# Message stage of a graph network: when VectorE adds two finished pair sums, between or behind the products of the next two pairs

## Chip, cores and metric

The kernel runs on one core of a Trainium2 chip (trn2). The metric is the device time of one execution in microseconds, the median of several runs. Everything is float32 except a few small index helpers.

## The reference, cut to what matters

The program is a chain of four blocks on 3125 nodes with 256 features: a graph layer, a mixture of experts, a second graph layer (messages along 53125 edges), and a second mixture of experts, each added to its input. The change lies in the second graph layer alone:

```python
h = silu(edge_scalars @ fc_w1 * (1.0 / sqrt(NES))) * SILU_NORM
w_a, w_b, w_c, w_d = split(h @ fc_w2 * (1.0 / sqrt(FCN)), 4)     # 64 weights of each kind per edge
xg0, xg1 = y0[edge_src], y1[edge_src]                            # 64 scalars and 64 x 3 vectors of the source node
mid0 = w_a * xg0 * ea0
mid1 = w_b * einsum('euc,ec->eu', xg1, ea1) * INV_SQRT3
mid2 = (w_c * xg0)[:, :, None] * ea1[:, None, :]
mid3 = (w_d * ea0)[:, :, None] * xg1
agg = segment_sum(concatenate([mid0, mid1, mid2, mid3]), edge_dst)   # 53125 edges -> 3125 nodes
```

The edges are sorted by their destination. An earlier stage has stored the weights of each edge in DRAM (`edge_w`), and another the transformed node rows (`y_dram`).

## The kernel before

`sum_messages` (from L1865) is one of the kernel's stages. The nodes are cut into 25 tiles of 125, the edges into 208 blocks of 256 (`NB`), 128 partitions with two edges each. A **pair** is one block together with one tile into which some of its edges go; there are 232 pairs (`NPAIR`), since a block that straddles two tiles makes two. A **step** `s` handles pairs `2s` and `2s+1`, so there are 116 steps (`NST`), and five engines work on them at once:

- **GpSimd (POOL)**, L1936 to L1948: gathers the source rows, two indirect DMAs per block (L1940), 416 in all, into a ring of 32 blocks (`got`). Behind every second block it waits for the landing of two blocks that it issued earlier and adds two to `blocks_in` (L1934). Block `b` waits for `made >= (b - 6) // 2` (L1938).
- **SP**, L1907 to L1917: loads the edge weights of both pairs into one of four buffers `w`, behind `made` and `scaled_made` of the step that last used it.
- **ScalarE (ACT)**, L1954 to L1963: twelve scaled copies of the step's mask (L1961).
- **TensorE (PE)**, L1968 to L1984: sixteen float32 matmuls per step (four at L1978, twelve at L1982; the profile lists two records for each) that sum the products of each pair into one of six PSUM banks `ps_z`. It waits for `scaled_made`, for `made`, and for the sums of step `s-3` to have been added (`added`), because those free the banks.
- **VectorE (DVE)**, L2030 to L2048, in order, in iteration `s`: the mask of step `s+1` (L1993, which waits until PE has finished step `s-3`); the six products of step `s` (`products`, L2000: for each pair one instruction at L2010 and two at L2012), behind a wait for the weights, for both blocks (`blocks_in` against `need[1]`, L2004) and for PE; then the two additions of step `s-3` into `agg` (`add_sum`, L2016, the instruction at L2022). Each addition waits for the one before it (`added`, L2019), since both may go to the same tile.

Two registers per iteration hold the tiles to which the sums go, and two more the blocks that the next step reads (`value_load`, L1998 and L2037). The sequencer of VectorE loads them ahead of the instructions that need them; it also carries out the waits that stand in front of an instruction.

The lines that the change and the prediction speak of are L1934, L1938, L1940, L1978, L1982, L1993, L2000 to L2014 and L2016 to L2045.

Of the kernel before, what the change touches and what calls it, by code (L numbers as in the profile page):

```python
# [25 lines left out]
KC = 2  # L26
# [13 lines left out]
MUL = 64  # L40
# [5 lines left out]
ALU, ACT, AX = mybir.AluOpType, mybir.ActivationFunctionType, mybir.AxisListType  # L46
ds = bass.ds
# [100 lines left out]
def row(buf, at, lo=0, hi=None, parts=P):  # L148

    return buf[0:parts, ds(at, 1), lo:hi].rearrange("p o d -> p (o d)")  # L150
# [1714 lines left out]
def sum_messages(nc, k):  # L1865


    RING, LAG = 32, 3
# [3 lines left out]
    RS, MB, ZB, XB = 4, 4, 6, 3  # L1872
# [3 lines left out]
    NST = NPAIR // 2  # L1876
    assert NST * 2 == NPAIR
    with Phase(nc, "msg") as ph:
        FACTOR = C_X / math.sqrt(20.0) / math.sqrt(2 * MUL)
        raw, raw_zero, raw_in = k.up_w, ph.sem("raw_zero"), ph.sem("raw_in")  # L1880
        got = ph.sb("got", [128, RING, KC, 4, MUL])
        lent, used = k.x_sb[:, G:T, :].rearrange("p t d -> p (t d)"), [0]

        def borrow(n):
# [14 lines left out]
        w_in, got_in, blocks_in = ph.sems("w_in", RS), ph.sems("got_in", RING), ph.sem("blocks_in")  # L1899
        rest, rested = ph.sb("rest", [128, 32]), ph.sem("rested")  # L1900
        masked, scaled_made, made, summed, added = (
            ph.sem(x) for x in ("masked", "scaled_made", "made", "summed", "added"))
        block = ph.ctx.enter_context(nc.Block())

        @block.sync
        def _(sp):
            for s in range(NST):  # L1907
                if s >= RS:
                    sp.wait_ge(made, s - RS + 1)
                    sp.wait_ge(scaled_made, s - RS + 1)  # L1910
                if s == 1:
                    sp.wait_ge(k.x_put, 32 * (NG - 1))
                for h in range(2):
                    n = 2 * s + h
                    need = sp.value_load(k.pair_need[0:1, n:n + 1], min_val=1, max_val=NB)
                    sp.dma_start(w[s % RS][:, KC * h:KC * h + KC, :].rearrange("p u w -> p (u w)"),
                                 k.edge_w[ds((need - 1) * SB, SB), :].rearrange("(p u) w -> p (u w)", u=KC)).then_inc(w_in[s % RS], 16)  # L1917
            sp.wait_ge(raw_zero, 1)
            w00, w01, w10, w11 = k.L1_gnn_lin2_w00, k.L1_gnn_lin2_w01, k.L1_gnn_lin2_w10, k.L1_gnn_lin2_w11
            for q, (wa, wb) in enumerate([(w00, w11), (w11, w11), (w01, w10), (w10, w10)]):  # L1920
                sp.dma_start(raw[0:MUL, q, 0:MUL], wa).then_inc(raw_in, 16)
                sp.dma_start(raw[MUL:128, q, MUL:128], wb).then_inc(raw_in, 16)
            sp.wait_ge(summed, LAST + 1)
            for i in range(1, NG):
                for a, b in SPANS:
                    sp.dma_start(k.x_sb[a:b, i * G:i * G + G, :], k.x_dram[i * W:i * W + W, :].rearrange("(j p) d -> p j d", p=P)[a:b, :, :])\
                      .then_inc(k.x_back[i], 16)
# [58 lines left out]
        @block.vector  # L1986
        def _(dve):
            def mask(s):
                if s == 1:
                    dve.wait_ge(k.x_put, 32 * (NG - 1))  # L1990
                if s >= MB:
                    dve.wait_ge(summed, s - MB + 1)
                dve.tensor_tensor(plain[s % MB][:, :, :], ps_lanes[:, :].unsqueeze(1).to_broadcast([128, CH, P]),  # L1993
                                  k.pair_dst[:, 2 * s:2 * s + 2, :].rearrange("p n u -> p (n u)").unsqueeze(2)
                                  .to_broadcast([128, CH, P]), ALU.is_equal).then_inc(masked, 1)

            def place(n):
                return dve.value_load(k.pair_need[0:1, n:n + 1], min_val=1, max_val=NB)  # L1998

            def products(s, need):  # L2000
                p = prod[s % XB]
                v = w[s % RS][:, :, 0:D].rearrange("p c (k v) -> p c k v", v=MUL)
                dve.wait_ge(w_in[s % RS], 32 * (s // RS + 1))
                dve.wait_ge(blocks_in, need[1])  # L2004
                if s >= XB:
                    dve.wait_ge(summed, s - XB + 1)
                for h in range(2):
                    y = got[:, ds(need[h] % RING, 1), :, :, :].rearrange("p o u k v -> p (o u) k v")
                    at = slice(KC * h, KC * h + KC)
                    dve.tensor_tensor(p[:, at, 0:8:7, :], v[:, at, 0:4:3, :], y[:, :, 0:1, :].to_broadcast([128, KC, 2, MUL]), ALU.mult)  # L2010
                    for q in (1, 2):
                        last = dve.tensor_tensor(p[:, at, 3 * q - 2:3 * q + 1, :], v[:, at, q:q + 1, :].to_broadcast([128, KC, 3, MUL]),  # L2012
                                                 y[:, :, 1:4, :], ALU.mult)
                last.then_inc(made, 1)  # L2014

            def add_sum(n, tile):  # L2016
                if n % 2 == 0:
                    dve.wait_ge(summed, n // 2 + 1)
                dve.wait_ge(added, 1 + n)  # L2019
                if n == 0:  # L2020
                    dve.wait_ge(rest_zero, 1)
                dve.tensor_tensor(row(k.agg, tile), ps_z[n % ZB][0:P, :, :].rearrange("p k v -> p (k v)"), row(k.agg, tile), ALU.add)\  # L2022
                   .then_inc(added, 1)

            dve.memset(raw[:, :, :], 0.0).then_inc(raw_zero, 1)
            dve.wait_ge(lanes_made, 1)
            dve.memset(k.agg[:, 0:T // 2, :], 0.0).then_inc(added, 1)
            mask(0)
            need = [place(0), place(1)]
            for s in range(NST + 3):  # L2030
                if s + 1 < NST:
                    mask(s + 1)
                if s < NST:
                    products(s, need)
                if s >= 3:
                    first, second = 2 * s - 6, 2 * s - 5
                    tile = [dve.value_load(k.pair_tile[0:1, n:n + 1], min_val=0, max_val=T - 1) for n in (first, second)]  # L2037
                if s + 1 < NST:
                    need = [place(2 * s + 2)]
                if s >= 3:  # L2040
                    add_sum(first, tile[0])
                if s + 1 < NST:
                    need.append(place(2 * s + 3))
                if s >= 3:
                    add_sum(second, tile[1])  # L2045
                if s == NST - 1:
                    dve.wait_ge(raw_in, 128)
                    dve.tensor_scalar(k.up_w[:, :, :], raw[:, :, :], FACTOR, None, ALU.mult)  # L2048
# [520 lines left out]
```

## Time and profile before

| what | us |
|---|---|
| median of three timed runs | 1999.07 |
| lowest and highest of them | 1993.88, 2004.77 |
| span of the profiled execution | 2413.3 |
| message stage in the profiled execution, 1248 to 2058 | 810 |
| stage of the first graph layer in it, 75 to 725 | 650 |

The profiled execution is one run in which each instruction is recorded; its span, from the first to the last instruction, is 414 us longer than the median of the timed runs, which are not recorded. Durations of single instructions and the order of events are read from it; how its length stands to the timed runs has to be argued. In the profile's rows "idle before" is the time the engine stood still in front of an instruction, and the name behind the arrow is what ended it: an engine with its line, "issue" where nothing in the profile held it, "remote" where the signal came from no instruction that the profile could match.

### The profile page before, as it was taken

What the parts mean: (1) busy time and instruction counts of PE and PEld (TensorE: products, weight loads), DVE (VectorE), ACT (ScalarE), POOL (GpSimd) and SP (SyncE); (2) the same over time, 40 slices, a digit from 0 to 9 for tenths busy, and PEclk for the clock granted to TensorE, in tenths of its full rate; (3) what the DMA queues carried; (4) which work ended last, traced back from release to release, by engine and by line L of the source; (5) the groups of instructions that cost most, each with busy time, mean ns of one, the idle gap of its engine ahead of it and who ended that gap; (6) DMA issues with size and microseconds to landing.
All of it is one profiled execution on the core that took longest, in us unless ns stands there. A gap on an engine that the chain in (4) does not pass through costs nothing. (4 is left out here: it accounts for less than half of the span.)

```text
span 2413.3 us, 38460 instructions
## 1 busy us (share of the span) xinstructions
PE 1891.3 (78%) x9911; PEld 1517.9 (63%) x9911; DVE 1125.8 (47%) x2791; ACT 1021.4 (42%) x3052; POOL 1104.5 (46%) x1499
## 2 busy tenths in 40 slices
PE   1368787877799858999455877787778789899699
PEld 1245454554466657999335766676767679777588
DVE  3532222222242374544664666565656669431322
ACT  2513343343353532333264555454545557454222
POOL 5547667666700004555375665565655550000243
PEclk7679999889999858999777888887888889999799
DMA  5636556565734026666544554555554553255553
GB/s 150 202 90 198 190 187 198 185 193 187 210 140 138 11 64 201 212 212 215 135 149 147 150 159 140 151 155 145 147 153 144 150 148 107 69 164 177 155 180 129
DMA packets 229197, 376.43 MB, mean 156 GB/s; under 512 B 66081, under 2 KB 114308, under 8 KB 228998
## 3 DMA queue, kind: packets, MB, share of 16 engines
q1 hardware_dynamic: 174820, 222.13, 31.0%
q0 software_dynamic: 52224, 150.15, 20.2%
q8 instruction: 89, 1.46, 0.2%
q10 hardware_dynamic: 1954, 1.79, 0.2%
q14 instruction: 110, 0.90, 0.1%
HBM read 275.38 MB, written 99.57 MB: 155 GB/s over the span
## 5 line engine op out<-in xcount | busy, mean ns | idle before, releaser
L1940 POOL DMA_INDIRECT msg_got<-y_dram,block_src x416 | 412.4, 991 | 293.5 <-DVE msg_prod L2012 139.7
L439 POOL DMA_INDIRECT ffn_w<-xn_dram,block_src x384 | 364.6, 949 | 219.2 <-issue 81.7
L1961 ACT ACTIVATE msg_scaled<-msg_plain,msg_w 128x125 f32<-128x125 f32 x1044 | 314.0, 386 | 280.1 <-DVE msg_plain L1993 234.6
L554 PE MATMUL sum_ps_bank<-ffn_w,sum_onehot 128*125 x928 | 270.5, 419 | 115.6 <-DVE sum_onehot L893 84.3
L554 PEld LDWEIGHTS sum_ps_bank<-ffn_w,sum_onehot 128*125 128x125 f32 x928 | 184.0, 206 | 264.6 <-issue 246.6
L881 DVE TENSOR_TENSOR agg<-sum_ps_bank,agg 125x256 f32 x232 | 98.4, 424 | 432.4 <-PE sum_ps_bank L554 216.5
L541 PE MATMUL sum_ps_bank<-sum_fc,sum_space 128*128 128x512 f32 x416 | 231.9, 644 | 68.9 <-ACT sum_space L639 48.3
L650 ACT ACTIVATE sum_space<-sum_ps_bank,sum_rec 128x128 f32<-128x128 f32 x416 | 131.0, 369 | 330.4 <-PE sum_ps_bank L541 159.5
L1982 PE MATMUL msg_ps_z<-msg_prod,msg_scaled 128*125 128x128 f32 x1416 | 207.5, 293 | 53.7 <-issue 53.0
L1982 PEld LDWEIGHTS msg_ps_z<-msg_prod,msg_scaled 128*125 128x125 f32 x1416 | 198.6, 206 | 72.4 <-issue 64.1
L2022 DVE TENSOR_TENSOR agg<-msg_ps_z,agg 125x512 f32 x232 | 159.4, 687 | 23.9 <-issue 5.2
L1978 PE MATMUL msg_ps_z<-msg_prod,msg_plain 128*125 128x256 f32 x472 | 142.1, 420 | 31.9 <-issue 20.0
L2439 POOL DMA_INDIRECT last_rows<-ffn_rows,ffn_token x32 | 30.8, 963 | 289.2 <-SPq L78 279.7
L1533 ACT ACTIVATE ffn_run_hid<-ffn_run_ps_h,cols 128x128 f32<-128x128 f32 x256 | 73.2, 368 | 178.9 <-issue 134.6
L1993 DVE TENSOR_TENSOR msg_plain<-msg_ps_lanes,pair_dst 128x500 f32<-128x500 f32 x87 | 58.5, 672 | 190.6 <-remote 183.6
L1961 ACT ACTIVATE x_sb<-x_sb 128x125 f32<-128x125 f32 x348 | 104.0, 385 | 93.4 <-DVE x_sb L1993 77.2
L541 PEld LDWEIGHTS sum_ps_bank<-sum_fc,sum_space 128*128 128x128 f32 x416 | 76.0, 205 | 93.5 <-ACT sum_space L639 53.8
L1490 PEld LDWEIGHTS ffn_run_ps_h<-ffn_run_rows_t,ffn_run_w 128*128 128x128 f32 x1024 | 125.9, 194 | 5.0 <-DVE ffn_run_rows_t L1575 1.8
L1490 PE MATMUL ffn_run_ps_h<-ffn_run_rows_t,ffn_run_w 128*128 128x128 f32 x1024 | 126.6, 277 | 1.0 <-DVE ffn_run_rows_t L1575 1.0
L1982 PE MATMUL msg_ps_z<-x_sb,msg_scaled 128*125 128x128 f32 x672 | 100.1, 292 | 29.9 <-issue 29.7
L1504 PE MATMUL ffn_run_ps_r<-ffn_w,ffn_run_hid 128*128 x512 | 121.0, 379 | 0.0
L2012 DVE TENSOR_TENSOR msg_prod<-msg_w,msg_got 128x384 f32<-128x384 f32 x236 | 120.2, 550 | 0.0
(343 smaller groups left out, 3397.9 us busy)
## 6 DMA issues: line engine op xcount, KB each, us to landing
edge_w<-sum_space SPq DMA_DIRECT2D x52, 1040.0 KB
msg_w<-edge_w SPq DMA_DIRECT2D x174, 260.0 KB
ffn_run_w<-in_L_ffn_w SPq DMA_DIRECT2D x64, 512.0 KB
x_sb<-edge_w SPq DMA_DIRECT2D x58, 260.0 KB
ffn_rows<-agg SPq DMA_DIRECT2D x25, 448.0 KB
ffn_w<-in_L_ffn_w SPq DMA_DIRECT2D x16, 512.0 KB, 8.7
wd<-in_L_ffn_Wd SPq DMA_DIRECT2D x8, 1024.0 KB, 8.6
msg_got<-y_dram,block_src POOLq DMA_INDIRECT x416
```

Source lines behind the costliest of these rows:

```text
L439: pool.indirect_dma_start(got[:, (b + 1) % RING, u, :], None, k.x if b < RAW else k.xn_dram, bass.IndirectOffsetOnAxis(ap=k.block_src[:, b ...
L541: pe.matmul(ps_w[q % WB][:, :, :].rearrange("p u d -> p (u d)"), hid[g % 2][:, b, :], fc2[:, :, :, :].rearrange("p u k v -> p (u k v)"), s ...
L554: last = pe.matmul(ps_sum[n % ZB][0:P, :], onehot[n % OB][:, u, :], got[:, ds(need % RING, 1), u, :].rearrange("p o d -> p (o d)"), start= ...
L650: act.activation(to[:, b, u, 0:128], ps_w[q % WB][:, u, 0:128], ACT.Copy, scale=r[:, b, u, 8:9])
L1490: last = pe.matmul(ps_h[b][c // 4][:, c % 4, :], w1[s][:, q, c * 128:(c + 1) * 128], rows_t[b][:, q, :], start=(q == 0), stop=(q == 1))
L1504: last = pe.matmul(ps_r[b][:, :], hid[b][:, c, :], m.w2[:, ds(e, 1), c, :].rearrange("p o d -> p (o d)"), start=(c == 0), stop=(c == HC - 1))
L1940: pool.indirect_dma_start(got[:, (b + 1) % RING, u, :, :].rearrange("p k v -> p (k v)"), None, k.y_dram, bass.IndirectOffsetOnAxis(ap=k.bl ...
L1961: last = act.activation(scaled[s % MB][:, x, c, :], plain[s % MB][:, c, :], ACT.Copy, scale=w[s % RS][:, c, D + x:D + x + 1])
L1978: pe.matmul(z[0:P, 0:4, :], mask[:, c, :], p[:, c, 0:4, :], start=(u == 0), stop=False, skip_group_check=True)
L1982: last = pe.matmul(z[0:P, 4:6 + x:1 + x, :], by[:, x, c, :], p[:, c, 4 + x:8:3 - x, :], start=False, stop=(x == 2 and u == KC - 1), skip_g ...
L2012: last = dve.tensor_tensor(p[:, at, 3 * q - 2:3 * q + 1, :], v[:, at, q:q + 1, :].to_broadcast([128, KC, 3, MUL]), y[:, :, 1:4, :], ALU.mult)
L2022: dve.tensor_tensor(row(k.agg, tile), ps_z[n % ZB][0:P, :, :].rearrange("p k v -> p (k v)"), row(k.agg, tile), ALU.add)\
```

## The change

In each iteration VectorE does the mask, the three products of the first pair, the first addition, the three products of the second pair, and the second addition. Before, it did the mask, all six products, and both additions. The wait for the gathered blocks is split: the first pair's products wait for the first pair's block, the second pair's products for the second's. The registers that name the next step's blocks are both loaded behind the products, where before one stood ahead of each addition. The signal `made` comes, as before, from the last product of the second pair. No arithmetic instruction is added or taken away.

```diff
-            def products(s, need):
+            def products(s, need, h):
                 p = prod[s % XB]
                 v = w[s % RS][:, :, 0:D].rearrange("p c (k v) -> p c k v", v=MUL)
-                dve.wait_ge(w_in[s % RS], 32 * (s // RS + 1))
-                dve.wait_ge(blocks_in, need[1])
-                if s >= XB:
-                    dve.wait_ge(summed, s - XB + 1)
-                for h in range(2):
-                    y = got[:, ds(need[h] % RING, 1), :, :, :].rearrange("p o u k v -> p (o u) k v")
...
-                last.then_inc(made, 1)
+                if h == 0:
+                    dve.wait_ge(w_in[s % RS], 32 * (s // RS + 1))
+                    if s >= XB:
+                        dve.wait_ge(summed, s - XB + 1)
+                dve.wait_ge(blocks_in, need)
+                y = got[:, ds(need % RING, 1), :, :, :].rearrange("p o u k v -> p (o u) k v")
...
+                if h == 1:
+                    last.then_inc(made, 1)
...
                 if s < NST:
-                    products(s, need)
+                    products(s, need[0], 0)
                 if s >= 3:
                     first, second = 2 * s - 6, 2 * s - 5
                     tile = [dve.value_load(k.pair_tile[0:1, n:n + 1], min_val=0, max_val=T - 1) for n in (first, second)]
-                if s + 1 < NST:
-                    need = [place(2 * s + 2)]
                 if s >= 3:
                     add_sum(first, tile[0])
+                if s < NST:
+                    products(s, need[1], 1)
                 if s + 1 < NST:
-                    need.append(place(2 * s + 3))
+                    need = [place(2 * s + 2), place(2 * s + 3)]
                 if s >= 3:
                     add_sum(second, tile[1])
```

## Rows read from the trace of the kernel before

**Rows 1.** Span and granted TensorE clock of the core.

```profile
core 0: 2413.3 us, clock 0.875
```

**Rows 2.** Waits of DVE in the message stage, 1248 to 2058 (total, times, longest).

```profile
DVE msg_plain L1993 <- remote: 183.6, 32, 18.9
DVE x_sb L1993 <- remote: 63.6, 12, 7.1
...
DVE agg L2022 <- issue: 5.2, 7, 2.2
```

**Rows 3.** Waits of DVE in the first graph layer, 75 to 725.

```profile
DVE agg L881 <- remote: 162.5, 36, 6.3
```

**Rows 4.** Timeline of PE (start, length, engine, line, operation, count, [idle before]).

```profile
1522.60 1.03 PE L1978 MATMUL msg_ps_z<-x_sb,msg_plain 128*125 128x256 f32 x4
...
1524.77 1.03 PE L1978 MATMUL msg_ps_z<-x_sb,msg_plain 128*125 128x256 f32 x4
...
1526.95 1.03 PE L1978 MATMUL msg_ps_z<-msg_prod,msg_plain 128*125 128x256 f32 x4
...
1530.14 0.27 PE L1982 MATMUL msg_ps_z<-msg_prod,msg_scaled 128*125 128x128 f32 x1 [1.16 <-issue]
1531.57 0.27 PE L1982 MATMUL msg_ps_z<-msg_prod,msg_scaled 128*125 128x128 f32 x1 [1.16 <-issue]
```

**Rows 5.** Timeline of DVE over one iteration, after the last gather.

```profile
1984.55 0.68 DVE L2022 TENSOR_TENSOR agg<-msg_ps_z,agg 125x512 f32 x1
1985.38 0.69 DVE L2022 TENSOR_TENSOR agg<-msg_ps_z,agg 125x512 f32 x1
1985.99 0.67 DVE L1993 TENSOR_TENSOR msg_plain<-msg_ps_lanes,pair_dst 128x500 f32<-128x500 f32 x1
1986.58 0.41 DVE L2010 TENSOR_TENSOR msg_prod<-msg_w,msg_got 128x256 f32<-128x256 f32 x1
...
1987.85 0.41 DVE L2010 TENSOR_TENSOR msg_prod<-msg_w,msg_got 128x256 f32<-128x256 f32 x1
...
1989.12 1.52 DVE L2022 TENSOR_TENSOR agg<-msg_ps_z,agg 125x512 f32 x2
1990.56 0.67 DVE L1993 TENSOR_TENSOR msg_plain<-msg_ps_lanes,pair_dst 128x500 f32<-128x500 f32 x1
```

**Rows 6.** Timeline of POOL: the stage's first gather, then blocks at full pace.

```profile
1248.67 1.04 POOL L1940 DMA_INDIRECT msg_got<-y_dram,block_src  x1 [3.06 <-POOLq L82]
...
1965.37 0.95 POOL L1940 DMA_INDIRECT msg_got<-y_dram,block_src  x1 [0.17 <-issue]
...
1967.88 0.95 POOL L1940 DMA_INDIRECT msg_got<-y_dram,block_src  x1 [0.17 <-issue]
```

**Rows 7.** Timeline of DVE: the first three steps, and the end of the stage.

```profile
1257.32 0.42 DVE L2010 TENSOR_TENSOR msg_prod<-msg_w,msg_got 128x256 f32<-128x256 f32 x1 [0.89 <-issue]
...
1261.60 0.42 DVE L2010 TENSOR_TENSOR msg_prod<-x_sb,msg_got 128x256 f32<-128x256 f32 x1 [1.06 <-issue]
...
1266.81 0.43 DVE L2010 TENSOR_TENSOR x_sb<-msg_w,msg_got 128x256 f32<-128x256 f32 x1 [1.99 <-issue]
...
2045.37 0.41 DVE L2010 TENSOR_TENSOR msg_prod<-msg_w,msg_got 128x256 f32<-128x256 f32 x1
...
2055.43 1.53 DVE L2022 TENSOR_TENSOR agg<-msg_ps_z,agg 125x512 f32 x2 [1.37 <-PE msg_ps_z L1982]
```

**Rows 8.** Timeline of POOL and DVE: gathers beside products.

```profile
1957.11 1.34 POOL L1940 DMA_INDIRECT msg_got<-y_dram,block_src  x1 [0.17 <-issue]
1957.54 0.42 DVE L2010 TENSOR_TENSOR msg_prod<-x_sb,msg_got 128x256 f32<-128x256 f32 x1
1957.87 1.02 DVE L2012 TENSOR_TENSOR msg_prod<-x_sb,msg_got 128x384 f32<-128x384 f32 x2
```

**Rows 9.** POOL's groups by line (count, busy us, mean ns, idle before).

```profile
L1940 POOL DMA_INDIRECT msg_got<-y_dram,block_src x416 | 412.4, 991 | 293.5 <-DVE msg_prod L2012 139.7 <-issue 90.4 <-DVE x_sb L2012 59.9
L439 POOL DMA_INDIRECT ffn_w<-xn_dram,block_src x384 | 364.6, 949 | 219.2 <-issue 81.7 <-remote 56.7 <-PE sum_ps_bank L554 51.1
```

More of the change, by code:

```diff
@@ L1998, in place @@
                 return dve.value_load(k.pair_need[0:1, n:n + 1], min_val=1, max_val=NB)
-            def products(s, need):
+            def products(s, need, h):
                 p = prod[s % XB]
                 v = w[s % RS][:, :, 0:D].rearrange("p c (k v) -> p c k v", v=MUL)
-                dve.wait_ge(w_in[s % RS], 32 * (s // RS + 1))
-                dve.wait_ge(blocks_in, need[1])
-                if s >= XB:
-                    dve.wait_ge(summed, s - XB + 1)
-                for h in range(2):
-                    y = got[:, ds(need[h] % RING, 1), :, :, :].rearrange("p o u k v -> p (o u) k v")
[L2009 to L2013, printed above, removed]
-                last.then_inc(made, 1)
+                if h == 0:
[4 more added lines that the diff above has]
+                y = got[:, ds(need % RING, 1), :, :, :].rearrange("p o u k v -> p (o u) k v")
+                at = slice(KC * h, KC * h + KC)
+                dve.tensor_tensor(p[:, at, 0:8:7, :], v[:, at, 0:4:3, :], y[:, :, 0:1, :].to_broadcast([128, KC, 2, MUL]), ALU.mult)
+                for q in (1, 2):
+                    last = dve.tensor_tensor(p[:, at, 3 * q - 2:3 * q + 1, :], v[:, at, q:q + 1, :].to_broadcast([128, KC, 3, MUL]),
+                                             y[:, :, 1:4, :], ALU.mult)
+                if h == 1:
+                    last.then_inc(made, 1)
             def add_sum(n, tile):
```

## The prediction

> **What bounds the kernel now.** I read the span first [rows 1], then who held VectorE in the stage that changes, then single iterations in the order of time. The profiled execution took 2413.3 us, 414 us more than the median of the timed runs, so before anything is costed it must be clear where those 414 us sit. VectorE was held in front of its mask 44 times, 247.2 us in all, by signals that no instruction explains [rows 2], and in the first graph layer 36 times for 162.5 us in the same way [rows 3]. Together that is 409.7 us, and 2413.3 - 409.7 = 2003.6 us, 0.2% above the timed median of 1999.07.
>
> What happens in such a hold shows on TensorE. Normally it goes through a pair in 2.17 us, 4.35 us a step (starts at 1522.60, 1524.77, 1526.95) [rows 4]. In a hold its matmuls start 1.43 us apart, with nothing to wait for (1530.14 and 1531.57) [rows 4]. Then VectorE, whose mask needs the step that TensorE finished three steps ago, stands still. I read the holds as a cost of being recorded, because the sum above then closes; that is an inference, not something the rows state. I therefore cost the change on the steps without holds, as a difference, and subtract it from the timed median.
>
> In a step without holds VectorE is the slowest engine of those that the rows show. Late in the stage an iteration takes 1990.56 - 1985.99 = 4.57 us with no idle time in it [rows 5]: mask to products 0.59, the first pair's products 1.27, the second pair's 1.27, both additions 1.44. TensorE needs 4.35. GpSimd needs 2.51 us for a block (1965.37 to 1967.88) [rows 6], and 208 blocks for 116 steps make 208 x 2.51 / 116 = 4.50 us a step. So three engines lie within 5% of each other, and that closeness decides this case.
>
> **The change, part by part.**
>
> The additions. The first starts 0.83 us ahead of the second, but the second only 0.61 us ahead of the mask that follows it (starts at 1984.55, 1985.38, 1985.99) [rows 5]. The operations are alike; the difference of 0.22 us is the second addition waiting until the first has ended, and that wait also holds all that is queued behind it on VectorE. With 1.27 us of products in between, the first addition is over long before the second is due, so the wait goes. An iteration becomes 0.59 + 1.27 + 0.61 + 1.27 + 0.61 = 4.35 us. Both additions stand in the 113 iterations from 3 to 115 that have products, so VectorE alone gives back 113 x 0.22 = 24.9 us.
>
> Here a rule speaks against the change. The Trainium skill (VectorE: DVE Perf Modes, "The DRAIN you can't avoid") says that a chain of VectorE operations takes the same time with a semaphore behind each as with one behind the last. By that rule splitting the additions gives 0 us in place of 24.9. The 0.83 against 0.61 us does not agree with it, but a chain of two additions from PSUM that the rows show nowhere without a wait leaves it a chance.
>
> What comes in the way next. TensorE at 4.35 us a step is level with the new iteration, so 24.9 us is also the most that it lets through. GpSimd at 4.50 is not level. Its first gather starts at 1248.67 [rows 6]. Two blocks later, at 1253.7, the first products can't start before 1257.32 [rows 7], so arrival and signal take about 3.6 us. Without holds the last blocks come in at 1248.67 + 522.1 + 3.6 = 1774.4. From the start of the last step's products to the end of the last addition the trace has 2055.43 + 1.53 - 2045.37 = 11.6 us [rows 7]. So the gathers allow no end before 1786.
>
> VectorE's own end, before the change: 1257.3, then 115 x 4.57 us less three iterations without additions (3 x 1.44), 521.2 us, then 11.6 us, is 1790.1. To this come its waits for blocks at the start, 1.06 and 1.99 us at steps 1 and 2 [rows 7]. They go on until tile boundaries give VectorE pairs without a new block, since two blocks take 5.02 us against 4.57. I allow 3 to 9 us, the upper end an estimate: some thirteen more waits of 0.45 us. That is 1793 to 1799. After the change VectorE alone would end near 1771, but the gathers at 1786. The gain is then 7 to 13 us and not 24.9.
>
> And the gathers may be slower. A gather whose end falls into the products is stretched, 1.34 us where 0.95 is usual [rows 6, 8]. On average one of this stage takes 991 ns against 949 in the first layer [rows 9]: 416 x 0.042 = 17.5 us. If they are stretched as often without holds, the gathers end at 1803, are the bound already before the change, and faster additions give nothing. So the gathers leave between 0 and 13 us. I take 7, since both ends rest on equally near rows.
>
> The split wait for blocks. It now stands behind the first addition and holds the second pair's products, the second addition and the next mask; TensorE waits for these. Before, it stood ahead of all of these and the first pair as well. Where blocks are late, the new place lets 1.27 + 0.61 us of work go ahead; at a bound that stays with the gathers this only shortens the last step, at most 1.9 us once. I count 0 to -2.
>
> `made` comes 0.61 us later in the iteration. Three engines wait for it. TensorE waits for the second addition anyway, which is still the iteration's last instruction. SP's loads of weights are issued three steps ahead of their use, some 13 us, and no DMA moves otherwise. GpSimd's block 8 is due at 1248.67 + 8 x 2.51 = 1268.8 and needs the first `made`, near 1259.9; that is 9 us of cover. Without it each step would wait 0.61 us longer. Cost 0.
>
> The register loads. All four stay. Two now stand between the second pair's products and the second addition, under 1.27 us of queued products. VectorE's additions stood still for "issue" 5.2 us in all [rows 2], so a worse place costs some us at most: 0, with +5 as the bound.
>
> Sum: -7 us, from 1999.07 to **1992**; by the bounds, -15 to +5.
>
> **The rivals.**
>
> 1. The gathers keep ahead and all of VectorE's 24.9 us arrives: 1974. For it: while recorded GpSimd mostly waits for VectorE [rows 9]. Against it: its 2.51 us per block are an unhindered pace, the same as in the first layer's mean of 949 ns, and a ring of 32 blocks gives no pace.
>
> 2. Slower. The products hold GpSimd, and in the new order they come in two groups of 1.27 us, each meeting other gathers. Products fill 2.54 of 4.35 us instead of 2.54 of 4.57. If the two cycles lock so that every gather is stretched by 0.084 us on average, twice what the rows show, the gathers take 17.5 us more and end at 1820 instead of 1803: 2016 where they were the bound before, 2009 on the middle of what I took. It decides as soon as the mean stretch passes about 0.06 us. For it: the stretched gather [rows 8] lies under products. Against it: an addition now stands between the groups, so no gather meets more than three products in a row. The Trainium skill (SBUF — State Buffer, "Who interferes with whom") says that a VectorE instruction with two SBUF inputs contends with a GpSimd instruction that reads SBUF; the 1.34 us under products agrees, and by it an addition, with one input in PSUM, lets GpSimd through.
>
> 3. The change does not do what it says: the 0.22 us is no wait but goes with every addition, or TensorE is late by as much. Time 1999. Against it: the second addition, the same operation, is followed after 0.61 us.
>
> **How the numbers follow.** The forecast, that gathers take over as the bound after some us, has 0.55, with its own range 1985 to 1999. Rival 1 has 0.16, rival 2 0.12, rival 3 0.17. This kernel's measurement can tell about 0.5%, 10 us, from no change. Faster than 1989: rival 1 and the far end of the forecast (some 0.15), 0.31. Slower than 2009: half of rival 2, 0.06, and 0.01 for the rest, 0.07. In between 0.62. A range for 8 in 10 leaves out half of rival 1 and half of rival 2: 1975 to 2007.
>
> **What would show it.** In the trace after, in a step without holds: the first addition followed after 0.61 us by the second pair's products, and mask to mask 4.35 us where no block is awaited (without that the first step is wrong, and rival 3 right). Near 4.57 with idle time in front of products would name the gathers. The mean of L1940 decides rival 2: about 990 ns or less against 1030 and more. The forecast is wrong if the timed gain passes 15 us, for then the gathers were not the limit, or if the holds are not recording but part of every run; then TensorE paces the stage, and the change is worth nothing.

## The result, and the profile after

The change makes the kernel slower: 2013.76 us, median of 6 runs (2010.1 to 2022.41), against 1998.63 us before (6 runs). The ratio of their runs is 1.0093, with a 95% interval of 1.0069 to 1.0116 (the quotient of the two medians alone is 1.0076). By the medians that is 15.1 us more where 7 less were predicted, and 6.8 us above the top of the range.

The kernel before was recorded a second time (first experiment), and this recording has none of the holds of [rows 2, 3]. It is the one to compare with. Span and clock of the kernel after, then of the second recording of before:

```profile
core 0: 2009.9 us, clock 0.938
```

```profile
core 0: 1995.3 us, clock 0.937
```

The groups of GpSimd's gathers (line, count, busy us and mean ns, idle time), first of the kernel after:

```profile
L1940 POOL DMA_INDIRECT msg_got<-y_dram,block_src x416 | 435.7, 1047 | 100.7 <-issue 93.0 <-DMA msg_got<-y_dram,block_src 3.1 <-POOLq L82 3.0
L439 POOL DMA_INDIRECT ffn_w<-xn_dram,block_src x384 | 364.4, 949 | 97.2 <-issue 87.1 <-PE sum_ps_bank L554 5.7 <-DMA xn_dram<-xn 2.4
```

The same of the second recording of the kernel before:

```profile
L1940 POOL DMA_INDIRECT msg_got<-y_dram,block_src x416 | 417.0, 1002 | 100.7 <-issue 93.3 <-DMA msg_got<-y_dram,block_src 4.3 <-POOLq L82 3.0
```

The clock is the same, GpSimd's idle time is the same to a tenth of a us (100.7), and the first layer's gathers (L439) are at 949 ns as in [rows 9]. What changed is one number: a gather of the message stage takes 1047 ns in place of 1002. Over 416 gathers this is 435.7 - 417.0 = 18.7 us.

Now VectorE's waits in the message stage of the kernel after (what waited, for whom, total us, times, longest):

```profile
DVE msg_prod L2010 <- POOLq L1934: 23.4, 36, 1.5
DVE agg L2023 <- issue: 15.0, 63, 0.6
DVE x_sb L2010 <- POOLq L1934: 10.3, 14, 2.3
```

L1934 is where GpSimd reports that blocks have arrived. In the second recording of before, the same waits came to 2.2 and 2.0 us, with 9.4 us more in front of the products put down to "issue". So VectorE now stands in front of its products and waits for gathers. The "issue" line is that of both additions of an iteration, which stand on L2023 alike.

The timeline of VectorE and GpSimd in the kernel after shows both sides of it (start, length, engine, line, operation, [idle before]):

```profile
1301.73 0.69 DVE L2023 TENSOR_TENSOR agg<-msg_ps_z,agg 125x512 f32 x1 [0.19 <-issue]
1302.34 0.67 DVE L1993 TENSOR_TENSOR msg_plain<-msg_ps_lanes,pair_dst 128x500 f32<-128x500 f32 x1
...
1302.93 0.41 DVE L2010 TENSOR_TENSOR msg_prod<-x_sb,msg_got 128x256 f32<-128x256 f32 x1
1303.26 1.02 DVE L2012 TENSOR_TENSOR msg_prod<-x_sb,msg_got 128x384 f32<-128x384 f32 x2
1303.93 1.17 POOL L1940 DMA_INDIRECT msg_got<-y_dram,block_src  x1 [0.30 <-issue]
1304.20 0.68 DVE L2023 TENSOR_TENSOR agg<-msg_ps_z,agg 125x512 f32 x1
...
1305.40 0.95 POOL L1940 DMA_INDIRECT msg_got<-y_dram,block_src  x1 [0.17 <-issue]
1305.53 0.42 DVE L2010 TENSOR_TENSOR msg_prod<-x_sb,msg_got 128x256 f32<-128x256 f32 x1 [0.65 <-POOLq L1934]
1305.87 1.02 DVE L2012 TENSOR_TENSOR msg_prod<-x_sb,msg_got 128x384 f32<-128x384 f32 x2
1306.66 1.05 POOL L1940 DMA_INDIRECT msg_got<-y_dram,block_src  x1 [0.30 <-issue]
...
1307.69 0.67 DVE L1993 TENSOR_TENSOR msg_plain<-msg_ps_lanes,pair_dst 128x500 f32<-128x500 f32 x1
1308.02 0.95 POOL L1940 DMA_INDIRECT msg_got<-y_dram,block_src  x1 [0.17 <-issue]
...
1309.28 1.17 POOL L1940 DMA_INDIRECT msg_got<-y_dram,block_src  x1 [0.30 <-issue]
```

The change does what it says: no addition waits for the other, and the one at 1301.73 is followed by the mask 0.61 us later. But from mask to mask it is 1307.69 - 1302.34 = 5.35 us, with 0.65 us of waiting for a block in it. And the gathers fall into a beat: 1303.93, 1306.66 and 1309.28 each begin in the third product of a group of three and take 1.17, 1.05 and 1.17 us; those that begin under a mask or an addition, or in idle time (1305.40, 1308.02), take 0.95. Where no block is awaited, an iteration of this trace takes 4.33 us.

The stage from the first gather to the last addition closes the account. The rows of after, and behind them those of the second recording of before:

```profile
1076.08 1.04 POOL L1940 DMA_INDIRECT msg_got<-y_dram,block_src  x1 [3.04 <-POOLq L82]
...
1637.34 0.95 POOL L1940 DMA_INDIRECT msg_got<-y_dram,block_src  x1 [0.30 <-issue]
...
1650.09 1.53 DVE L2023 TENSOR_TENSOR agg<-msg_ps_z,agg 125x512 f32 x2 [1.16 <-PE msg_ps_z L1982]
```

```profile
1079.26 1.04 POOL L1940 DMA_INDIRECT msg_got<-y_dram,block_src  x1 [3.03 <-POOLq L82]
...
1621.73 0.96 POOL L1940 DMA_INDIRECT msg_got<-y_dram,block_src  x1 [0.30 <-issue]
...
1637.62 1.53 DVE L2022 TENSOR_TENSOR agg<-msg_ps_z,agg 125x512 f32 x2 [1.11 <-PE msg_ps_z L1982]
```

After: 1651.62 - 1076.08 = 575.5 us. Before: 1639.15 - 1079.26 = 559.9. The difference, 15.6 us, is the whole of the loss. It is 18.7 us more of gathering, less 3.2 us by which VectorE now ends sooner behind the last gather (13.3 us in place of 16.5).

### The profile page after: what moved, and what is told of

The parts are those of the page before. It is cut to its first block and busy times, and to the rows that moved or that the text cites. A ratio compares the mean times of both kernels' runs of the same rounds, so it can differ in the third digit from the quotient of the medians.

```text
span 2009.9 us, 38460 instructions
## 1 busy us (share of the span) xinstructions
PE 1749.4 (87%) x9911; PEld 1428.7 (71%) x9911; DVE 1122.7 (56%) x2791; ACT 1021.9 (51%) x3052; POOL 1127.5 (56%) x1499
## 5 line engine op out<-in xcount | busy, mean ns | idle before, releaser
L1940 POOL DMA_INDIRECT msg_got<-y_dram,block_src x416 | 435.7, 1047 | 100.7 <-issue 93.0
L439 POOL DMA_INDIRECT ffn_w<-xn_dram,block_src x384 | 364.4, 949 | 97.2 <-issue 87.1
L554 PEld LDWEIGHTS sum_ps_bank<-ffn_w,sum_onehot 128*125 128x125 f32 x928 | 172.0, 193 | 191.8 <-issue 176.1
L554 PE MATMUL sum_ps_bank<-ffn_w,sum_onehot 128*125 x928 | 254.3, 399 | 51.1 <-DVE sum_onehot L893 25.8
L541 PE MATMUL sum_ps_bank<-sum_fc,sum_space 128*128 128x512 f32 x416 | 211.5, 593 | 1.3 <-ACT sum_space L639 1.3
L1982 PEld LDWEIGHTS msg_ps_z<-msg_prod,msg_scaled 128*125 128x125 f32 x1416 | 174.4, 189 | 6.8
L1982 PE MATMUL msg_ps_z<-msg_prod,msg_scaled 128*125 128x128 f32 x1416 | 175.1, 274 | 0.0
L2023 DVE TENSOR_TENSOR agg<-msg_ps_z,agg 125x512 f32 x232 | 158.6, 684 | 17.5 <-issue 15.0
L1978 PE MATMUL msg_ps_z<-msg_prod,msg_plain 128*125 128x256 f32 x472 | 124.8, 387 | 30.4 <-DVE agg L2023 19.3
L1595 POOL DMA_INDIRECT ffn_results<-ffn_run_res,ffn_place x64 | 66.4, 1038 | 102.3 <-DVE ffn_run_res L1554 102.3
L2012 DVE TENSOR_TENSOR msg_prod<-msg_w,msg_got 128x384 f32<-128x384 f32 x236 | 120.7, 551 | 0.0
L2401 PE MATMUL last_ps_r<-wd,last_hid_t 128*128 x512 | 117.4, 383 | 0.0
L1978 PEld LDWEIGHTS msg_ps_z<-msg_prod,msg_plain 128*125 128x125 f32 x472 | 79.8, 189 | 41.9 <-issue 23.7
```

Source lines behind the costliest of these rows:

```text
L439: pool.indirect_dma_start(got[:, (b + 1) % RING, u, :], None, k.x if b < RAW else k.xn_dram, bass.IndirectOffsetOnAxis(ap=k.block_src[:, b ...
L541: pe.matmul(ps_w[q % WB][:, :, :].rearrange("p u d -> p (u d)"), hid[g % 2][:, b, :], fc2[:, :, :, :].rearrange("p u k v -> p (u k v)"), s ...
L554: last = pe.matmul(ps_sum[n % ZB][0:P, :], onehot[n % OB][:, u, :], got[:, ds(need % RING, 1), u, :].rearrange("p o d -> p (o d)"), start= ...
L1940: pool.indirect_dma_start(got[:, (b + 1) % RING, u, :, :].rearrange("p k v -> p (k v)"), None, k.y_dram, bass.IndirectOffsetOnAxis(ap=k.bl ...
L1978: pe.matmul(z[0:P, 0:4, :], mask[:, c, :], p[:, c, 0:4, :], start=(u == 0), stop=False, skip_group_check=True)
L1982: last = pe.matmul(z[0:P, 4:6 + x:1 + x, :], by[:, x, c, :], p[:, c, 4 + x:8:3 - x, :], start=False, stop=(x == 2 and u == KC - 1), skip_g ...
```

## The experiments

All times stand against the kernel before, run on the same chip (1995.7 to 1999.3 us). Each mean gather comes from one recorded execution.

| kernel | us | ratio | 95% | mean gather, ns |
|---|---|---|---|---|
| before_again | 1997.0 (one run) | | | 1002 |
| split_wait_only | 1993.82 | 0.9994 | 0.9979 to 1.0008 | 1001 |
| order_only | 2023.9 | 1.0149 | 1.0126 to 1.0171 | 1080 |
| the change | 2013.76 | 1.0093 | 1.0069 to 1.0116 | 1047 |
| before_psum | 1977.56 | 0.9919 | 0.9891 to 0.9946 | 949 |
| after_psum | 1973.36 | 0.9894 | 0.9874 to 0.9914 | 949 |
| before_half | 1986.41 | 0.9951 | 0.9931 to 0.9971 | 970 |
| after_half | 1960.84 | 0.9836 | 0.9809 to 0.9863 | 1596 |
| before_no_rest | 1991.25 | 0.9955 | 0.9933 to 0.9978 | 992 |
| after_no_rest | 2029.21 | 1.0156 | 1.0125 to 1.0187 | 1075 |
| mask_between | 2030.87 | 1.0154 | 1.0128 to 1.018 | 1084 |
| mask_between_no_rest | 2022.88 | 1.013 | 1.0096 to 1.0164 | 1075 |
| after_pad | 2006.58 | 1.0064 | 1.004 to 1.0089 | 1039 |

The theory after the result: the stage is now paced by gathers that are stretched by VectorE's products, and the change brings more of them under products at a bad moment (rival 2 of the prediction). The rivals: the split wait and its signals cost the time; or VectorE's own gain was never there.

**The kernel before, once more.** No edit.

> The kernel before, profiled once more, because its first profile held VectorE for 247 us in the message stage by signals that nothing explains, and the profile after the change shows no such holds. Theory (the gathers set the pace, and the new order stretches them more): without holds the gathers of L1940 run without waiting for VectorE, their mean lies near 1010 ns against 1047 after the change (15 us less over 416), and VectorE waits for blocks here too. Rival (VectorE set the pace before, and the new order costs VectorE time of its own): mask to mask 4.57 us nearly everywhere, no waits for blocks after the first steps, and the gathers' mean about as after the change.

Measured: 1997.0 us, mean gather 1002 ns, no hold by "remote" anywhere in the stage. From about the tenth step on most iterations take 4.57 us (with those of 4.58, 85 of 115), the pace of a VectorE that waits for nothing. But the gathers run from 1079 to 1623 with nothing but their usual pauses, VectorE stands 13.6 us in all in front of its products, and the stage ends only 16.5 us behind the last gather. The two were level. In the kernel after, where gathers set the pace, the stage ends 13.3 us behind the last gather; so with the gathers as they were, only some 3 us were there to win.

**Which half of the change costs.** The order alone, with both blocks awaited ahead of the first pair, and the split wait alone in the old order:

```diff
-                dve.wait_ge(blocks_in, need)
+                if h == 0:
+                    dve.wait_ge(blocks_in, both)
```

> The new order, but the products of the first pair wait for both blocks, as before the change; the second pair's wait falls away. Theory (more stretching of the gathers by the new places of the products): still slower than before, 2005 to 2020 us, with a mean of L1940 above that of before. Rival (the split wait is the cost, since the wait behind the first addition holds the second addition and the next mask): no slower than before, 1990 to 2000 us.

```diff
-                dve.wait_ge(blocks_in, need[1])
...
                 for h in range(2):
+                    dve.wait_ge(blocks_in, need[h])
```

> The old order, but the first pair's products wait for the first block alone and the second pair's for the second. Theory (stretching by the new places of the products): within 5 us of before, 1994 to 2003 us. Rival (the split wait is the cost): most of the 15 us here, 2008 to 2016 us.

Measured: the order alone costs more than the whole change (ratio 1.0149, mean gather 1080 ns); the split wait alone is worth nothing that can be told from zero (0.9994, 1001 ns). In the new order the split wait gives back some 10 us, the difference of 1.0149 and 1.0093. So it is the order, and the split wait is no cause of the loss.

**Gathers without contention.** The products read a PSUM tile in place of the gathered rows. Waits, order and gathers are unchanged:

```diff
-                y = got[:, ds(need % RING, 1), :, :, :].rearrange("p o u k v -> p (o u) k v")
+                fixed = ps_lanes[:, 0:MUL].unsqueeze(1).unsqueeze(1)
...
-                                             y[:, :, 1:4, :], ALU.mult)
+                                             fixed.to_broadcast([128, KC, 3, MUL]), ALU.mult)
```

> The new order, with one operand of all six products read from PSUM (the lane numbers, which lie there anyway) in place of the gathered rows in SBUF, so that each product has only one input in SBUF; the messages are then not those of the reference. Gathers, waits and the number and size of all instructions stay. Theory (products with both inputs in SBUF hold the gathers up): the mean of L1940 falls from 1047 to about 950 ns, a block takes 2.51 us again, and the time falls by 25 to 40 us, to 1975 to 1990. Rival (the gathers are slow for another reason, the DMA traffic or the number of instructions): the mean stays above 1020 ns and the time within 8 us of that after the change.

> Old order, the products read PSUM in place of the gathered rows (the messages are not the reference's), so that no gather is stretched: 2.51 us a block, gathers over 521 us after the first. VectorE at 4.57 is the bound: 1985 to 1995, between 12 and 22 us above the new order with the same edit (1973). That would say that the change is right in sign wherever gathers aren't stretched, as the prediction's forecast had it. If instead both orders are level with PSUM operands, the stretch is not what turned the sign.

The gathers' group, and then a stretch of the timeline, of the new order with PSUM operands:

```profile
L1940 POOL DMA_INDIRECT msg_got<-y_dram,block_src x416 | 394.9, 949 | 101.1 <-issue 88.4 <-DMA msg_got<-y_dram,block_src 7.5 <-POOLq L82 3.2
```

```profile
1406.08 1.01 DVE L2012 TENSOR_TENSOR msg_prod<-msg_w,msg_ps_lanes 128x384 f32<-128x384 f32 x2
1406.17 0.95 POOL L1940 DMA_INDIRECT msg_got<-y_dram,block_src  x1 [0.30 <-issue]
```

The gather at 1406.17 begins 0.09 us into a product and still takes 0.95; of all 416 only the first takes more than 0.97. The mean falls to 949 ns, exactly that of the first layer, and the time by 40 us against the change. The products themselves keep their length to a few ns (547 against 549 at L2012, medians). That shows the cause: products that read the gathered rows from SBUF stretch the gathers, and products that read PSUM in their place don't. The Trainium skill (SBUF — State Buffer, "Who interferes with whom") says that a VectorE instruction with two SBUF inputs contends with a GpSimd instruction that reads SBUF; the runs agree, since a gather reads its row numbers (`block_src`) there, and they add the price. The edit also takes the gathered tile itself out of the products; no run reads another SBUF tile in its place, so that it is the second SBUF operand as such, whichever tile it is, was not shown by a run.

The old order with the same edit came in at 1977.56, lower than the 1985 to 1995 expected, because the old order had waited for stretched gathers as well: the sum of its iterations falls from 537.4 to 522.3 us, nearly all of them but the first ten at 4.54. Of these 15 us some 3.5 are the 0.03 us by which an iteration without waits is shorter here, in both orders. The new order is ahead by 4.2 us, which the two intervals don't separate; in the two recordings, from the first gather to the last addition, it is 544.4 against 534.7 us. By the expectation's own words orders that come out level would mean that the stretch did not turn the sign. That does not follow: with the stretch gone, the new order's loss of 15 us is gone. Whether the gain of 7 us that was forecast stands in its place is not shown by the timed runs; the recordings have the sign and about the size.

**VectorE without a gather bound.** From block 32 on only one of a block's two gathers runs, in both orders:

```diff
-                for u in range(KC):
+                for u in range(KC if b < RING else 1):
```

> Old order; from block 32 on only the first of a block's two gathers runs, so the messages are not the reference's, and GpSimd has some 1.5 us of work a block in place of 2.5. VectorE at 4.57 us a step is then alone in setting the stage's end: 1980 to 1992 us, mask to mask 4.57 in nearly all iterations.

> New order, the second gather of a block left out from block 32 on, as in the old order's run. With the gathers off the path the spacing of the additions is worth what the prediction worked out, 113 x 0.22 = 25 us against the same run in the old order: 1955 to 1967, mask to mask 4.33 to 4.35. If VectorE's gain itself is smaller, or TensorE at 4.35 us a step lets less through, the difference is under 15 us.

Measured: 1986.41 and 1960.84, a difference of 25.6 us (by the two intervals uncertain by some 7) against 24.9 in the prediction. Two masks in a row and two gathers from the new order's timeline, and the gathers' groups of the old order and of the new:

```profile
1395.01 0.66 DVE L1993 TENSOR_TENSOR msg_plain<-msg_ps_lanes,pair_dst 128x500 f32<-128x500 f32 x1
...
1399.34 0.66 DVE L1993 TENSOR_TENSOR msg_plain<-msg_ps_lanes,pair_dst 128x500 f32<-128x500 f32 x1
1399.95 2.15 POOL L1940 DMA_INDIRECT msg_got<-y_dram,block_src  x1 [0.17 <-issue]
1402.40 1.57 POOL L1940 DMA_INDIRECT msg_got<-y_dram,block_src  x1 [0.17 <-issue]
```

```profile
L1940 POOL DMA_INDIRECT msg_got<-y_dram,block_src x240 | 232.7, 970 | 212.2 <-DVE msg_prod L2012 118.0 <-DVE x_sb L2012 58.7 <-issue 30.0
```

```profile
L1940 POOL DMA_INDIRECT msg_got<-y_dram,block_src x240 | 383.0, 1596 | 48.8 <-issue 43.2 <-POOLq L82 3.1 <-DMA msg_got<-y_dram,block_src 1.8
```

An iteration takes 4.33 us, 100 times of 115, and TensorE lets it through. In the old order with this edit nearly all take 4.57. This is the cleanest reading of the case: VectorE's gain is real and whole. In the same trace the gathers are the worst of all runs, 1596 ns, and it costs next to nothing, because 176 of the 416 are gone. What a stretched gather costs depends on whether gathers set the pace.

**Is it the two groups, or any faster iteration?** In mask_between all six products stay together, and the mask of the next step is put between the additions:

```diff
-                if s + 1 < NST:
-                    mask(s + 1)
                 if s < NST:
                     products(s, need)
...
                     add_sum(first, tile[0])
                 if s + 1 < NST:
+                    mask(s + 1)
```

> The spacing of the two additions by another operation: six products together behind one wait for both blocks as in the old order, then first addition, mask of the next step, second addition. The 0.22 us between the additions goes as in the new order, but the products are not split. If the splitting of the products is what stretches the gathers, the mean of a gather stays near 1000 ns and the time falls by 0 to 20 us, 1975 to 1997. If any shorter VectorE iteration locks the products onto the gathers (the products start when a block arrives), the mean rises to 1040 ns or more and the time to 2010 or more.

Measured: 2030.87, the slowest of all, with a mean gather of 1084 ns. Iterations that wait for nothing take 4.33 us here too. Four rows of GpSimd:

```profile
1136.14 0.95 POOL L1940 DMA_INDIRECT msg_got<-y_dram,block_src  x1 [0.30 <-issue]
1137.39 2.45 POOL L1940 DMA_INDIRECT msg_got<-y_dram,block_src  x1 [0.17 <-issue]
1140.15 0.95 POOL L1940 DMA_INDIRECT msg_got<-y_dram,block_src  x1 [0.30 <-issue]
1141.40 2.77 POOL L1940 DMA_INDIRECT msg_got<-y_dram,block_src  x1 [0.17 <-issue]
```

The gather of 1137.39 ends at 1139.84, some 0.9 us after the last of the six products gave way to an addition at 1138.93: it waited for the whole rest of the run of products. So products in two groups are not the only arrangement that stretches the gathers, and a group of six can do worse. By its expectation this result speaks for a shorter iteration as such; the next run asks whether the shorter iteration is needed.

In after_pad the new order gets a small memset behind the second addition, so that its iteration is about as long as the old one:

```diff
+                if s + 1 < NST:
+                    if s >= 1:
+                        dve.wait_ge(padded, s)
+                    dve.memset(pad[:, :], 0.0).then_inc(padded, 1)
```

> New order with a memset of some 0.2 us behind the second addition of each iteration, on data that nothing reads: VectorE's iteration is as long as in the old order, about 4.57 us. If the loss comes from a VectorE that is faster than the gathers and so starts its products whenever blocks arrive, the padded order falls back to about the old time, 1995 to 2003, with a mean gather near 1000 ns. If the arrangement itself, products in two groups, stretches the gathers, the mean stays at 1040 ns or more and the time at 2010 or above.

Measured: 2006.58, mean 1039 ns, most iterations that don't wait at 4.48 us (the mask starts 0.14 us into the memset, so the padding is worth 0.15 us a step). The time fell between what the two theories expected, and the mean just below what the second did. The mean speaks for the arrangement: much nearer the old pace than that of the change, the gathers are still stretched about as in it. The time against the change is not told apart, 1.0064 and 1.0093 with intervals that overlap. No run has the new order at the full 4.57 us, so what a shorter iteration adds stays open.

**A faster GpSimd?** The small memset between two blocks, and the wait for it, are left out in three orders:

```diff
-                if b >= 1:
-                    pool.wait_ge(rested, b)
-                pool.memset(rest[:, :], 0.0).then_inc(rested, 1)
```

> Old order, without the small memset on GpSimd and the wait for it between two blocks (a block should take some 2.2 us in place of 2.51). If VectorE's 4.57 us a step paces the old order, as the second recording of the old kernel shows from about the tenth step on, only the first steps gain: 1985 to 1995 us, mask to mask still 4.57. If the gathers pace the old order, the whole 0.3 us a block shows until VectorE is met: about 1975 or less. The mean of a gather should stay near 1000 ns or rise a little, since VectorE's products take the same share of time.

> New order, without the small memset on GpSimd and the wait for it between two blocks. If the new order loses because stretched gathers became the bound (562 us for 208 blocks, 2.70 us each), taking some 0.3 us from each block gives 2.40 us, 4.30 us a step, below VectorE's 4.35: VectorE becomes the bound, about 1970 to 1980 us, 20 us below the same edit in the old order, and the sign of the change turns. If the loss lies elsewhere (signal paths of the second wait, TensorE's later start), the time stays at 2005 to 2014 and the difference between the orders stays as it was, +15.

> First addition, mask, second addition behind six products, and GpSimd without the small memset between blocks. If the gathers' pace is what keeps the shorter iteration from paying, it pays here: about 1970 to 1980 us, level with the new order without the memset. If the stretch grows with the faster pace and takes the 0.3 us back, 1990 or more.

All three expectations rest on a pace of 2.2 us a block, and that is not what came. GpSimd's gathers in the new order without the memset:

```profile
1314.80 0.94 POOL L1940 DMA_INDIRECT msg_got<-y_dram,block_src  x1 [0.30 <-issue]
1316.05 0.95 POOL L1940 DMA_INDIRECT msg_got<-y_dram,block_src  x1 [0.30 <-issue]
1317.30 0.97 POOL L1940 DMA_INDIRECT msg_got<-y_dram,block_src  x1 [0.30 <-issue]
```

The pause in front of a gather is 0.30 us with the memset (0.14 of work and 0.17 of idle time) and without it, so a block still takes 2.51 us and the theories weren't put to the test. What the runs do show: an edit that leaves the pause as it was moved the new order from 2013.76 to 2029.21 and the mean gather from 1047 to 1075 ns. Where the gathers lie against the products is a matter of tenths of a us. In the old order the same edit is worth 0.45%, 1991.25 us, and that kernel is faster than the kernel before and than the change. This lies in the expected range, but the faster pace from which the range was worked out did not come; the mean gather went from 1002 to 992 ns. mask_between without the memset, 2022.88, is not told apart from mask_between by the intervals.

## Why the prediction was wrong, step by step

**Held.** The holds were not part of a normal run: the second recording has none, and its span of 1995.3 is near the 2003.6 that the sum of [rows 1 to 3] left. An iteration of VectorE without waits takes 4.33 us where 4.35 was worked out from [rows 5], and with the gathers out of the way this is worth 25.6 us against 24.9. Rival 3 fell with it. The rule of the Trainium skill (VectorE: DVE Perf Modes, "The DRAIN you can't avoid"), taken in the prediction to mean that the split would bring nothing, is not borne out by 4.57 against 4.33 us. TensorE went along at 4.33. Undisturbed gathers take 521.5 us from first to last in after_psum, 522.1 in the prediction.

**Failed.** The step is the one that begins "And the gathers may be slower". It took the stretch of [rows 9], 0.042 us a gather, as a property of the gathers that the change leaves alone, and so as a cost that is in both sums. It is a property of where the gathers lie against the products. The change moved the products, and the stretch went from 1002 - 949 = 53 to 1047 - 949 = 98 ns. The mechanism was written down as rival 2, with a doubling as its price, 17.5 us, and 2009 to 2016 as its time; measured were 18.7 us and 2013.76. The doubling had been assumed, not worked out, so that the size came out is luck. What was wrong was its chance of 0.12, and the reason given against it: that an addition between the groups lets the gathers through.

The same step says that a gather is stretched whose end falls into the products. The first recording of the kernel before, from which [rows 8] come, has a gather that ends under products, at 1956.81, and takes 0.95:

```profile
1955.86 0.95 POOL L1940 DMA_INDIRECT msg_got<-y_dram,block_src  x1 [0.30 <-issue]
1956.27 0.41 DVE L2010 TENSOR_TENSOR msg_prod<-x_sb,msg_got 128x256 f32<-128x256 f32 x1
1956.60 1.02 DVE L2012 TENSOR_TENSOR msg_prod<-x_sb,msg_got 128x384 f32<-128x384 f32 x2
```

The gather of [rows 8], at 1957.11, begins in the second of the two products from 1956.60 on; that is what counts. In the second recording of before and in that of after, a gather that begins outside the products takes 0.97 us at most (the stage's first, 1.04, aside), though 110 and 160 of them end under one.

The rows of the second recording of the kernel before show what the reason against rival 2 overlooked:

```profile
1395.35 1.02 DVE L2012 TENSOR_TENSOR x_sb<-x_sb,msg_got 128x384 f32<-128x384 f32 x2
1395.42 1.31 POOL L1940 DMA_INDIRECT msg_got<-y_dram,block_src  x1 [0.17 <-issue]
1396.29 0.42 DVE L2010 TENSOR_TENSOR x_sb<-x_sb,msg_got 128x256 f32<-128x256 f32 x1
1396.63 1.02 DVE L2012 TENSOR_TENSOR x_sb<-x_sb,msg_got 128x384 f32<-128x384 f32 x2
1397.04 0.97 POOL L1940 DMA_INDIRECT msg_got<-y_dram,block_src  x1 [0.30 <-issue]
1397.57 0.68 DVE L2022 TENSOR_TENSOR agg<-msg_ps_z,agg 125x512 f32 x1
```

The gather of 1395.42 begins 0.07 us into a product. That product hands over to the next 0.47 us after its start (two of them from 1395.35 to 1396.29), at 1395.82, and the gather ends 0.91 us later: it waited for the change of products. With the pause of 0.30 the next one starts 1.22 us after the release, and three products take 1.27 us; it starts 0.06 us before the next change and takes 0.97. So in a run of six products one gather pays and the next rides along. In the new order the additions stand after every third product, and each group can make a gather pay. That account is argued from rows, not shown by a run that moves only the phase.

Counted over the whole timelines, about as many gathers begin under a product in both orders, 228 before and 229 after (of some 410 between the first product and the last addition). But before, 158 of them take less than 1.0 us, all but one because they begin in the last 0.11 us of a product; after, only 55 do, and 31 of these begin so late. Over 1.04 us take 69 gathers before and 164 after. The old order lay well; that is what the 0.042 us of [rows 9] had measured.

A better figure was to be had from the rows. If gathers began at random moments, one would wait on average for the rest of the product that it meets: with products that follow each other after 0.33 us ([rows 8]) and twice 0.47 (the rest of the 1.27 of [rows 5]), twice in 4.35 us, the estimate is (2 x 0.33 x 0.33 + 4 x 0.47 x 0.47) / (2 x 4.35) = 0.13 us a gather. The old order paid 0.05, the change 0.10, order_only and mask_between 0.13. The forecast should have asked why the old order paid so little, and reckoned with a move towards 0.13, which would have put the gathers at 54 us of stretch in place of 17.5.

**Mis-sized.** What the gathers leave: 7 us were taken, and by the recordings it was some 3 even with the stretch as it had been (16.5 - 13.3). The split wait: it was counted at 0 to -2; alone in the old order it measured -4 to +2 (0.9979 to 1.0008), which allows that, but in the new order it gives back some 10, by shorter gathers (1080 to 1047 ns). The register loads, without weight: 0 was taken with a bound of 5 us, and the two additions now stand 15.0 us in front of "issue", 63 times, about half of it at each. Those at the second addition come mostly where blocks are awaited (the one at 1301.73 stands behind products that had waited 0.65 us); where VectorE doesn't wait for blocks both nearly vanish, 1.7 us in after_half.

**What stays open.** Why the new order settles at 1047 ns, order_only at 1080, and after_no_rest at 1075 was not settled; nor why some gathers wait for the next change of products and others for the end of the whole run, which happens 8 times in the change and 165 times in after_half; in the change, gathers that begin at the same place in a product do either.

## What to carry to other kernels

When two engines are level, the price that one adds to the other belongs in the sum on both sides of a change, and it moves with the phase: take for the new order what random phases would give, not what the old order happened to pay. Before spending an engine's gain, take the suspected bound away in both orders (half of the gathers here): it told in two runs that the gain was 25.6 us and that something else took 41. And a VectorE operation with one input in PSUM left the gathers alone, so the place of an operand is worth a trial in a stage that gathers; here it was tried only with a wrong operand.

## What was not expected of the hardware

- In the orders before and after, most gathers that begin early enough in a product end some 0.9 us after the next change of operations (1.05 to 1.37 us where 0.95 is usual). Others are held until the whole run of products is over: 1.57 and 2.15 us beside three (165 of the 240 in after_half), 2.45 and 2.77 beside six.
- The pause between two gathers is 0.30 us whether or not GpSimd has a memset of 0.14 us to do in it.
- One recording of a kernel may carry 410 us of holds that the timed runs don't have: 2413.3 us in [rows 1], 1995.3 in the second recording of the same kernel.
